# Other chunk positions for a norm's transpositions and its apply, and its statistics ahead of the combines, in a four-image metaformer kernel

## The reference, cut to what matters

```python
x = x + conv0(_ln_c(x))                     # deformable-attention block, x is (4, 96, 56, 56) f32
t = _to_tokens(x);  t = t + moe(_ln_t(t))   # 4 experts, hidden 384, top 2, gelu
x = _from_tokens(t, x)
x = x + conv1(_ln_c(x))                     # depthwise 7x7 + 5x3 + 3x5 + (1x7,7x1) + (1x5,5x1)
t = _to_tokens(x);  t = t + moe(_ln_t(t))
x = _from_tokens(t, x)

def _ln_t(v):                               # _ln_c: the same over the channels of a pixel
    return (v - mean(v)) / sqrt(var(v) + eps)

def moe(x):
    probs = softmax(x @ gate_w + gate_b); keep the 2 largest, divide by their sum
    h = gelu(x @ w1[e] + b1[e]);  y[e] = h @ w2[e] + b2[e]      # all 4 experts
    return sum over e of gate[e] * y[e]
```

## Time and profile before

| | |
|---|---|
| median of 3 runs | 1855.65 us (1854.15 to 1859.1) |
| profiled execution | 1861.07 us, span 1859.3 us |
| TensorE busy | 1400.2 us, 75% of the span |
| VectorE busy | 1346.9 us, 72% |
| ScalarE busy | 724.0 us, 39% |
| GpSimd busy | 303.3 us, 16% |
| mean granted TensorE clock | 0.911 |
| chain that ended last, by engine | PE 32%, DVE 29%, issue 8%, POOL 6%, ACT 3% |

### The profile page before, as it was taken

The page is one execution under the profiler, slowest core; times in us unless marked ns, Lnnn a source line. Parts: engine busy times, 40 slices in busy tenths (PEclk is TensorE's granted clock), DMA queues, the critical chain, the costliest instruction groups (busy, mean ns, idle before and its releaser), DMA issues.

```text
span 1859.3 us, 21000 instructions
## 1 busy us (share of the span) xinstructions
PE 1400.2 (75%) x5452; PEld 890.5 (48%) x5452; DVE 1346.9 (72%) x3073; ACT 724.0 (39%) x1436; POOL 303.3 (16%) x304
## 2 busy tenths in 40 slices
PE   2121623469879787787997899869987998899898
PEld 1010222335545454545554565546654665566565
DVE  1689398448874698547999799979998899443332
ACT  2130223225543354433444344434444344455443
POOL 1014013301150013201121112202121001000000
PEclk9999955589899899898998899989998999899999
DMA  2522213132421425123121421142213111221111
GB/s 66 130 53 59 74 45 90 37 109 68 118 75 30 139 67 145 56 83 93 58 62 42 149 68 56 45 146 61 66 49 113 45 52 42 79 70 60 53 59 48
DMA packets 105037, 137.66 MB, mean 74 GB/s; under 512 B 46070, under 2 KB 97144, under 8 KB 104184
## 3 DMA queue, kind: packets, MB, share of 16 engines
q1 hardware_dynamic: 98344, 131.20, 24.0%
q0 software_dynamic: 3072, 4.82, 1.1%
q10 hardware_dynamic: 3536, 0.63, 0.2%
HBM read 96.99 MB, written 39.62 MB: 73 GB/s over the span
## 4 chain that ended last, share of the span: by engine, by line
PE 32%; DVE 29%; issue 8%; POOL 6%; ACT 3%; DMA 1%; DVEq 1%; ACTq 0%; POOLq 0%
PE y_ps L815 15%; DVE acc L1106 9%; DVE part L1020 4%; PE h_ps L833 3%; PE h_ps L835 3%; PE h_ps L834 3%; POOL ln_rstd L730 3%; PE at_ps L920 3%; DVE ln_stats L994 3%; ACT ln_tok L598 2%; PE at_ps L851 2%; DVE pair L1026 2%; POOL ln_bias L733 2%; DVE ln_mv L1001 2%; PE lb_ps L794 1%
## 5 line engine op out<-in xcount | busy, mean ns | idle before, releaser
L629 ACT ACTIVATE hidden<-h_ps,b 128x448 f32<-128x448 f32 x672 | 421.5, 636 | 625.5 <-PE h_ps L835 619.5
L815 PE MATMUL y_ps<-hidden,w 128*96 128x448 f32 x1344 | 647.0, 567 | 19.1 <-ACT hidden L629 18.7
L1106 DVE SCALAR_TENSOR_TENSOR acc<-xq,all_w,acc 128x756 f32<-128x756 f32 (+2 forms) x504 | 475.9, 998 | 10.4 <-DMA xq<-norm_c 10.4
L833 PE MATMUL h_ps<-xh,w1h 96*128 96x448 f32 (+1 forms) x672 | 474.7, 706 | 0.0
L730 POOL TENSOR_TENSOR ln_rstd<-ln_ve,minus_half 112x4 f32<-112x4 f32 x112 | 154.7, 1382 | 1370.8 <-DVE ln_ve L1005 1362.7
L1020 DVE SCALAR_TENSOR_TENSOR part<-y_ps,b,gate_t 96x448 f32<-96x448 f32 x224 | 151.7, 677 | 298.9 <-PE y_ps L815 265.1
L794 PE MATMUL lb_ps<-ident,ln_tok 112*96 112x112 f32 x448 | 80.0, 312 | 332.5 <-ACT ln_tok L598 332.5
L598 ACT ACTIVATE ln_tok<-lt_ps,ln_bias,ln_rstd 112x96 f32<-112x96 f32 x448 | 156.3, 429 | 356.1 <-POOL ln_bias L733 332.1
L815 PEld LDWEIGHTS y_ps<-hidden,w 128*96 128x96 f32 x1344 | 211.2, 170 | 138.7 <-ACT hidden L629 52.7
L834 PE MATMUL h_ps<-xl,w1h 96*128 96x448 f32 (+1 forms) x672 | 251.0, 374 | 0.0
L835 PE MATMUL h_ps<-xh,w1l 96*128 96x448 f32 (+1 forms) x672 | 250.0, 372 | 0.0
(11 more groups left out here) (114 smaller groups left out, 1133.0 us busy)
## 6 DMA issues: line engine op xcount, KB each, us to landing
gate_t<-gates_dram SPq DMA_DIRECT2D x112, 336.0 KB, 3.3
xq<-norm_c SPq DMA_DIRECT2D x16, 420.0 KB, 4.9
xq<-norm_a SPq DMA_DIRECT2D x16, 336.0 KB, 4.1
ln_x_c<-in_x SPq DMA_DIRECT2D x28, 168.0 KB, 2.4
norm_a<-ln_cm_c SPq DMA_DIRECT2D x28, 168.0 KB, 2.0
x_res<-in_x SPq DMA_DIRECT2D x4, 1176.0 KB, 9.5
value_pairs<-pixels SPq DMA_DIRECT2D x4, 1176.0 KB
x_attn<-x_res SPq DMA_DIRECT2D x4, 1176.0 KB, 6.2
```

Of the source, the lines that this page charges most:

```text
L629: act.activation(hidden[c % HID_RING][:, :], h_ps[c % H_BANKS][:, 0:TILE], ACT.Gelu, bias=b1[l][:, c:c + 1]).then_inc(gelu_done, 1)
L815: pe.matmul(y_ps[e % Y_BANKS][0:C, 0:TILE], w2[l][:, c, :], hidden[c % HID_RING][:, :], start=(j == 0), stop=(j == CPE - 1)).then_inc(hid_ ...
L833: pe.matmul(ps, hi, xh[:, cols], start=True, stop=False)
L1106: step(g, dve.scalar_tensor_tensor(dst, src, w, dst, ALU.mult, ALU.add))
```

## The change

Chunk positions and VectorE's orders change; no instruction of the computation is added or removed, and the shares of the taps still go with the names.

```diff
-        STAGES = {"c": dict(turn_in=2, apply=6, turn_back=7, move=8), "f": dict(turn_in=8, apply=11)}
+        STAGES = {"c": dict(turn_in=1, apply=5, turn_back=6, move=7), "f": dict(turn_in=7, apply=11)}
...
-        LAST_STAGES = {"c": dict(turn_in=3, apply=5, turn_back=6, move=7),
-                       "f": dict(turn_in=6, apply=9, turn_back=10, move=11, scores=CHUNKS)}
+        LAST_STAGES = {"c": dict(turn_in=1, apply=5, turn_back=6, move=7),
+                       "f": dict(turn_in=6, apply=10, turn_back=11, move=11, scores=CHUNKS)}
...
-            ORDER = ("combine0", "split", "normalize0", "combine1", "combine2", "normalize1", "combine3", "sum",
+            ORDER = ("normalize0", "combine0", "split", "combine1", "normalize1", "combine2", "combine3", "sum",
...
-            LAST_ORDER = ("combine0", "split", "normalize0", "combine1", "normalize1", "combine2", "combine3",
+            LAST_ORDER = ("normalize0", "combine0", "split", "combine1", "normalize1", "combine2", "combine3",
```

## The result

| | before | changed |
|---|---|---|
| median | 1855.32 us (4 runs, 1854.15 to 1859.1) | 1911.32 us (4 runs, 1908.95 to 1911.76) |
| ratio | | 1.0296 (1.0278 to 1.0313) |
| profiled execution, span | 1859.3 us | 1910.0 us |
| mean granted TensorE clock | 0.911 | 0.892 |
| GpSimd busy | 303.3 us | 368.0 us |

What follows compares the result with a forecast made beforehand. Middle steps were taken as full on VectorE, step 0 as set by a chain through turn_back. The terms summed to -34.5 us, giving 1821 us from the median of 1855.65; 8-in-10 range 1802 to 1850, the forecast's own 1812 to 1831.

Steps and rivals of the forecast that it cites:

- What bounds the kernel: Slot 6: middle steps full on VectorE at 25.30 us; step 0, 42.08 us, set by a chain through turn_back.
- Step 0: Slots 3 to 8: statistics run in the xq wait, TensorE's stall goes, combine0 2.6 us later; -24.1 us.
- Step 6: Slots 5 to 8: most of VectorE's 2.89 us wait for combine1's y goes; -8.3 us in sum.
- Middle steps: 15 full steps in slots 5 to 7: +0.1 us each with the apply's timing unchanged, +1.5 in sum.
- Rival B: Full steps: GpSimd's product takes 2.51 us, not 0.95, delaying later stages 1.56 a step; 1866 us, chance 0.09.
- rival C: Step 0: without stalls TensorE's clock stays up, so the gain is larger; 1806 us, chance 0.12.
- Step 5: Attention slots 2 to 4: earlier turn_back and f statistics hold up TensorE and sampling work; +8.7 us.
- small ones: Slot 1 step 4's gelu wait, -3.6 us; tenths a step in slots 2 to 4, steps 1 to 3, and slot 9, -8.7.

Runs made afterwards that it cites:

- e11: Kernel before, with the new order and new chunk positions in step 0 of each slot alone: 1829.7 us, ratio 0.9843.
- e10: Changed kernel with combine0's and combine1's tap shares exchanged in the large convolution's slots only, c apply and turn_back one chunk later: 1819.7 us, ratio 0.9792.
- e14: Changed kernel with tap shares altered so that no tap stands between the c statistics and combine0 in middle steps: 1930.7 us, ratio 1.0369.
- e6: Changed kernel with one memset of 480 columns on GpSimd between power and product: 1920.2 us, ratio 1.0349.
- e12: Changed kernel with one memset of 1440 columns on GpSimd between power and product: 1941.1 us, ratio 1.0432.
- e4: Changed kernel with the tap shares of combine0 and combine1 exchanged (20 and 6 for 6 and 20) in steps 1 to 6: 1833.4 us, ratio 0.9862.

## Why the prediction was wrong, by its own steps

- **What bounds the kernel.** Right: middle steps full on VectorE, step 0 set by the chain through `turn_back`. The middle step and the step 0 of the earlier trace rows were read correctly.
- **Step 0, forecast -24.1.** The mechanism was right. The size was near, in part by luck: for slots 4 to 7 the forecast had -15.5, the changed kernel measured -16.3 and e11 -21.2, and both have -4.6 in slot 8. Two parts of it were off and nearly cancelled in slot 6: the statistics don't run inside the wait for `xq`, so a wait of 2.38 us stayed, and combine0 was 1.1 us later, not 2.6 (in slot 7 it was 2.6, in slot 5 it was earlier than before).
- **Step 6, forecast -8.3.** The mechanism is right (e10: -2.7, -1.9, -1.6, -2.7, in sum -8.9), but the changed kernel had +2.6, with the product at 3.9 or 4.8 us in the steps 6 of slots 5 to 7.
- **Middle steps, forecast +1.5.** This is the step that failed. Its arithmetic of the places held: `turn_back` came 2.96 us behind the place forecast, which is the excess of the product. But the sentence "+0.1 a step with the apply's timing unchanged" took the product's 0.95 along to a place with other neighbours, where it took 3.9 or 4.8 us. The term measured +80.7.
- **Rival B had the mechanism and the place**, GpSimd's product behind combine0 and `split` and the f statistics queued behind `turn_back`, and it was given 0.09. Its price, 1.56 a step, was mis-sized twice: the product cost 2.96, and the clock after the stall 2.0 more. The rows of before hinted at both, the 2.51 us product and the clock of 0.55 behind a stall, though not at the size of the first. The clock I had entered only as a gain (rival C), although a new stall brings it as a loss. With 4.95 for 15 steps instead of 1.56 for 25, B would have stood at some 1895. The argument held against it, that taps let the product end in 0.95 in the middle steps, was read from the old place.
- **Step 5, forecast +8.7, small ones -12.3.** Step 5 cost 2.5 us in slot 3 and -0.3 in slot 4. The wait of 4.09 us in slot 1, step 4, is gone. Slot 9 gained 3.0 us, steps 1 to 3 of slots 3 and 4 together 0.5. All of slots 0 to 3 gained 7.6. These terms were too small to have mattered.

## What to carry to other kernels

When statistics or any other producer is moved up in one engine's order, look at what the next engine's small instructions will now run beside, and take their duration only from rows with the same neighbours; a single odd row (2.51 us among 45 of 0.95) is a warning of what the new place may cost, and here still too low. In a loop whose step is full, allow, beside a new wait on TensorE, for the matmuls behind it to run at 1.2 GHz: here that was 2.0 us on top of a wait of 5.15. Where two halves of a change need each other, try each alone: here either half cost as much as both.

## What the runs showed of the hardware that I had not expected

GpSimd's product on 4 columns, 0.20 us when VectorE stood still (e14), took 0.95 beside taps alone, and 3.9 to 4.8 with a combine ahead of it and a run of taps beside it. Its power, 1.01 us at its shortest, took 6.4 or 7.3 when a combine, `split` and six taps ran beside it (e14). Delaying the product's begin by 0.3 and by 1.1 us did not move its end in the run of taps (e6, e12). TensorE's clock fell to 0.50 of 2.4 GHz after one wait of 1.88 us and stayed at 1.00 after one of 2.23 us (e4); what distinguishes them stays open.
